# Cross-attention and mixture of experts on one core: two of four batches go sorted through DRAM and meet only their chosen experts, and all expert work moves to 128-token tiles with the weights as the moving operand

## The reference, cut to what matters

```python
# attention, per batch
q = ctx @ Wq.T + bq;  k = ctx @ Wk.T + bk            # 256x128 each
att = softmax(q @ k.T, axis=-1)                       # 256x256
x = x + layernorm(x) @ att.T
# experts, per token of all 4 batches
hs = layernorm(x)
probs = softmax(hs @ router_gate.T)                   # 8 experts
score, idx = top_k(probs, 2);  score /= sum(score)
inter = hs @ expert_gate_up[e]                        # 256 -> 256: gate and up interleaved
h = inter[1::2] * silu(inter[0::2])                   # 128
x = x + sum over the two chosen e: score_e * (h @ expert_down[e])
```

## Time and profile before

| | us |
|---|---|
| three runs | 113.2, 113.69, 115.03 |
| profiled execution | 112.85 |
| its span | 111.0 |
| PE busy | 99.6 (90% of the span) |
| DVE busy | 75.5 |
| ACT busy | 42.8 |
| POOL busy | 43.4 |
| DMA moved | 10.23 MB |

### The profile page before, as it was taken

How to read it: one execution, slowest core, us unless ns; L and a number is a source line. 1 busy time by engine, 2 the same in 40 slices (tenths; PEclk the granted TensorE clock), 3 DMA queues, 4 the chain that set the end, 5 groups by cost and what they waited for, 6 DMA issues and landing times.

```text
span 111.0 us, 1638 instructions
## 1 busy us (share of the span) xinstructions
PE 99.6 (90%) x544; PEld 82.2 (74%) x544; DVE 75.5 (68%) x196; ACT 42.8 (39%) x89; POOL 43.4 (39%) x46
## 2 busy tenths in 40 slices
PE   6997899559998839999999999999999999999960
PEld 6884585346876637988988787898998998988950
DVE  1169969879965299989999599728963563553750
ACT  3355986745346244642090603234033033034200
POOL 3005045527000419999279360740440440440400
PEclk9999999999999995899999999999999999999998
DMA  2999993000003980000000000397050000000005
GB/s 67 264 265 336 361 348 113 0 0 0 6 0 111 320 334 0 6 0 0 0 0 0 0 0 4 127 360 279 0 189 0 6 0 0 0 0 0 0 5 184
DMA packets 8167, 10.23 MB, mean 92 GB/s; under 512 B 712, under 2 KB 7120, under 8 KB 8160
## 3 DMA queue, kind: packets, MB, share of 16 engines
q1 hardware_dynamic: 7744, 9.81, 26.9%
q10 hardware_dynamic: 416, 0.33, 0.9%
HBM read 9.05 MB, written 1.08 MB: 91 GB/s over the span
## 4 chain that ended last, share of the span: by engine, by line
PE 77%; DVE 9%; DMA 5%; ACT 4%; issue 1%; POOL 1%; DVEq 0%; ACTq 0%
PE ps_g L462 21%; PE ps_u L462 20%; PE ps_out L487 20%; DMA score_bc<-score_rows 4%; PE ps_out L440 3%; ACT probs L540 2%; PE ps_out L402 2%; PE ps_a L381 2%; DVE hs L643 2%; DMA score_rows<-scoresT 1%; DVE stats L628 1%; DVE x_sb L798 1%; DVE x_sb L683 1%; PE ps_u L373 1%; PE ps_u L421 1%
## 5 line engine op out<-in xcount | busy, mean ns | idle before, releaser
L341 POOL TENSOR_TENSOR h_lo<-h,h_hi 128x512 fp32r<-128x512 f32 x15 | 20.2, 1348 | 33.9 <-ACT h_hi L584 33.9
L808 DVE SCALAR_TENSOR_TENSOR scaled<-tanh_g,score_bc 128x512 f32<-128x512 f32 (+1 forms) x17 | 13.0, 770 | 15.5 <-ACT tanh_g L592 10.2
L592 ACT ACTIVATE tanh_g<-ps_g 128x512 f32<-128x512 f32 (+1 forms) x17 | 9.6, 571 | 28.4 <-PE ps_g L462 28.3
L487 PE MATMUL ps_out<-down_hi,h_lo 128*128 128x256 f32 x64 | 18.2, 285 | 0.0
L487 PE MATMUL ps_out<-down_lo,h_hi 128*128 128x256 f32 x64 | 18.0, 281 | 0.0
L487 PE MATMUL ps_out<-down_hi,h_hi 128*128 128x256 f32 x64 | 17.8, 279 | 0.0
L311 POOL TENSOR_TENSOR gu_lo<-gu_raw,gu_hi 128x512 fp32r<-128x512 f32 x8 | 10.5, 1310 | 11.3 <-ACT gu_hi L516 11.3
L584 ACT CAST h_hi<-h 128x512 fp32r<-128x512 f32 (+1 forms) x17 | 10.0, 591 | 10.9 <-DVE h L821 9.2
L821 DVE TENSOR_TENSOR h<-ps_u,gated 128x512 f32<-128x512 f32 (+1 forms) x17 | 11.1, 660 | 2.3 <-DVE gated L814 0.5
L487 PEld LDWEIGHTS ps_out<-down_hi,h_lo 128*128 128x128 f32 x64 | 12.2, 190 | 0.7
L487 PEld LDWEIGHTS ps_out<-down_lo,h_hi 128*128 128x128 f32 x64 | 12.2, 190 | 0.6
(11 more groups left out here) (147 smaller groups left out, 159.4 us busy)
## 6 DMA issues: line engine op xcount, KB each, us to landing
score_bc<-score_rows SPq DMA_DIRECT2D x8, 512.0 KB, 5.5
gu_raw<-_ffn_expert_gate_up_dram SPq DMA_DIRECT2D x4, 512.0 KB, 8.3
down_raw<-n_L_ffn_expert_down_dram SPq DMA_DIRECT2D x2, 512.0 KB, 8.6
out_dram<-x_sb SPq DMA_DIRECT2D x4, 256.0 KB, 2.2
ctx_sb<-in_ctx_dram SPq DMA_DIRECT2D x2, 256.0 KB, 3.5
x_sb<-in_x_dram SPq DMA_DIRECT2D x1, 512.0 KB, 6.7
x_sb<-in_x_dram ACTq DMA_DIRECT2D x1, 256.0 KB, 3.9
x_sb<-in_x_dram SPq DMA_DIRECT2D x1, 256.0 KB, 3.6
```

Source lines behind the costliest of these rows:

```text
L341: nc.gpsimd.tensor_tensor(h_lo[:, U % 2], h[:, U % 2], h_hi[:, U % 2].bitcast(f32), ALU.subtract).then_inc(h_lo_ready, 1)
L487: last = nc.tensor.matmul(dst, a[:, U % 2, cols], w[:, e], start=(e == 0 and i == 0 and j % 2 == 0), stop=(e == E - 1 and i == 2), skip_gr ...
L592: nc.scalar.activation(tanh_g[:, U % 2, part], ps_g[U % 2][:, part], ACT.Tanh, scale=0.5).then_inc(tanh_ready, 1)
L808: nc.vector.scalar_tensor_tensor(out=scaled[:, part], in0=tanh_g[:, U % 2, part], scalar=1.0, in1=score_bc[:, U // E, U % E, part], op0=AL ...
```

## The change

Batches 2 and 3 stay dense. Batches 0 and 1 (512 tokens, 4 tiles of 128) are sorted. After routing, TensorE counts for each token how many earlier tokens chose the same expert ("R": a strictly triangular and an all-ones matrix times the choices), DVE makes a row number for each token and choice, and 8 indirect DMAs of POOL scatter the rows of hs to `xs_rows` in DRAM. Every expert's rows begin at a tile of 128, so 15 tiles hold all 1,024 rows whatever the routing. SP loads the tiles, PE transposes them, and each tile meets the weights of the one expert that its number gives: PE reads 15 expert numbers into registers and addresses `W` by them. Results go to `ys_rows` in DRAM, 8 indirect DMAs of POOL gather them for each token, and DVE adds the two weighted rows (`combine`).

All expert work is now in groups of two 128-token tiles. The tokens are the stationary operand, and 256 columns of weights (gate beside up) move. The result has tokens on the partitions, so a dense score is a scalar per partition and the broadcast through DRAM is gone; but h has to be transposed before down (`transpose_h`). There are 24 groups: experts 0 to 3 of batches 2 and 3, then 8 groups of sorted tiles (the last has one tile), then experts 4 to 7 of both batches. Down of group k runs behind gate and up of group k+2, and the transposes of h(k+1) behind that.

The attention of all four batches now runs batch by batch ahead of the first expert group, except for H and the logits of batch 3. The logits come with tokens on the partitions from eight matmuls of 16 columns per batch. The remainders of down move from DVE and POOL to POOL alone.

```diff
+        FILLS = ["wq", "wk", "C0", "Q0", "K0", "C1", "E0", "Q1", "K1", "C2", "E1", "X0", "Q2", "K2", "C3", "A0", "E2",
+                 "gate", "M0", "X1", "A1", "Q3", "K3", "M1", "E3", "X2", "A2", "H0", "M2", "L0", "H1", "X3", "A3", "L1",
+                 "M3", "H2", "R", "L2", "H3", "L3"]
...
+        GROUPS = ([("dense", e, 2) for e in range(4)] + [("dense", e, 3) for e in range(4)]
+                  + [("sorted", s, None) for s in range(SG)]
+                  + [("dense", e, 2) for e in range(4, E)] + [("dense", e, 3) for e in range(4, E)])
...
+            def down_split(e):
...
+                nc.gpsimd.tensor_copy(W[:, e, 4], down_raw[:, e]).then_inc(down_hi_ready, 1)
+                pool.wait_ge(down_hi_ready, e + 1)
+                nc.gpsimd.tensor_tensor(W[:, e, 5], down_raw[:, e], W[:, e, 4].bitcast(f32),
+                                        ALU.subtract).then_inc(down_lo_ready, 1)
...
+            for j in range(ST):
+                for r in range(2):
+                    nc.gpsimd.indirect_dma_start(
+                        out=xs_rows, out_offset=bass.IndirectOffsetOnAxis(ap=slot[:, r, j:j + 1], axis=0),
+                        in_=hs[:, j], in_offset=None).then_inc(rows_scattered, 16)
+            for e in range(4, E):
+                gu_lo_part(e)
+                down_split(e)
+            for i in range(2):
+                pool.wait_ge(ys_stored[i], 16 * len(range(i, SG, 2)))
...
+            def load_experts():
+                pe.wait_ge(tile_expert_ready, 1)
+                for i in range(SLOT_TILES):
+                    experts.append(pe.value_load(tile_expert[0:1, i:i + 1], min_val=0, max_val=E - 1))
...
+                for t in range(group_tiles(k)):
+                    e = expert(k, t)
+                    terms = [(lo, half, c) for lo, half in ((0, 1), (0, 0), (1, 0)) for c in range(NT)]
+                    for i, (lo, half, c) in enumerate(terms):
+                        if kind == "dense":
+                            a = (hsT_hi, hsT_lo)[lo][:, b, c, t * P:(t + 1) * P]
+                        else:
+                            a = (xsT_hi, xsT_lo)[lo][:, n % 2, c, t]
+                        last = nc.tensor.matmul(dst[:, t * N:(t + 1) * N], a, W[:, e, 2 * half + c],
+                                                start=(i == 0), stop=(i == len(terms) - 1))
...
+            for k in range(NG + 2):
+                if k < NG:
+                    s = k + 1 - FIRST_SORTED
+                    if 0 <= s < SG:
+                        transpose_rows(s)
+                    gate_up_group(k)
+                if k == 0:
+                    att("H3")
+                if k == 1:
+                    att("L3")
+                if k >= 2:
+                    down_group(k - 2)
+                if 1 <= k <= NG:
+                    transpose_h(k - 1)
...
+            def combine(j):
+                dve.wait_ge(yg_in[j], 32)
+                nc.vector.scalar_tensor_tensor(out=part[:, j], in0=yg[:, 0, j], scalar=w_top[:, j, 0:1], in1=x1_sb[:, j],
+                                               op0=ALU.mult, op1=ALU.add).then_inc(part_ready, 1)
...
+            att("M0")
+            normalise_probs(2)
+            neg_mean_rstd(3)
+            att("K3")
+            normalise_x1(0)
+            att("M1")
+            att("E3")
+            att("H0")
+            normalise_x1(1)
+            normalise_probs(3)
+            att("M2")
+            att("L0")
+            att("H1")
+            normalise_x1(2)
+            att("L1")
+            route_sorted()
+            att("M3")
+            att("H2")
+            normalise_x1(3)
+            place_rows()
+            att("L2")
+            route_dense(1, 2)
```

More of the change, by code:

```diff
@@ new lines, in cross_attention_moe_kernel @@
+        w_is_top = sb("w_is_top", [P, 2, T - ST, E])
+        scores = sb("scores", [P, T - ST, E])
+        chosen = sb("chosen", [P, ST + 1, E])
+        over = sb("over", [P, E, E, ST])
+        first_tile = sb("first_tile", [P, E])
+        place = sb("place", [P, ST, E])
+        own_place = sb("own_place", [P, 2, ST, E])
+        slot_f = sb("slot_f", [P, 2, ST])
+        tile_expert_f = sb("tile_expert_f", [1, SLOT_TILES])
+        slot = sb("slot", [P, 2, ST], u32)
+        began = sb("began", [1, SLOT_TILES, E - 1])
@@ L613, in _ @@
-            split_h(UNITS - 1)
+            gap_exp(0, slice(0, ST))
+            split_gu(3)
+            hs_hi(2)
+            gap_exp(1, tiles(2))
+            for e in range(4, E):
+                split_gu(e)
+            for k in range(NG + 2):
+                s = k + 1 - FIRST_SORTED
+                if 0 <= s < SG:
+                    xt_hi(s)
+                if k == 1:
+                    hs_hi(3)
+                if k < NG:
+                    tanh(k)
+                if k == 2:
+                    gap_exp(2, tiles(3))
+                s = k - 2 - FIRST_SORTED
+                if 0 <= s < SG:
+                    evict_ys(s)
+                if 1 <= k <= NG:
+                    ht_hi(k - 1)
@@ new lines, in route_dense @@
+            def route_dense(i, b):
+                ts, ds = tiles(b), slice((b - SB) * LT, (b - SB + 1) * LT)
+                choose(ts, LT)
+                weights(i, ts, 0.5)
+                for r in range(2):
+                    step_on(nc.vector.tensor_tensor(w_is_top[:, r, ds], is_top[:, r, ts],
+                                                    w_top[:, ts, r:r + 1].broadcast_to([P, LT, E]), ALU.mult))
+                joined()
+                nc.vector.tensor_tensor(scores[:, ds], w_is_top[:, 0, ds], w_is_top[:, 1, ds], ALU.add).then_inc(scores_ready, 1)
@@ new lines, in _ @@
+            step_on(nc.vector.tensor_copy(tile_id[:], tile_no[:]))
+            step(nc.vector.tensor_copy(thr[:], thr_no[:]))
+            for e in range(E):
+                last = nc.vector.memset(thr[:, e, e:E], 1.0e6)
+                step_on(last)
+            joined()
+            att("gate")
+            att("M0")
[4 more added lines that the diff above has]
+            att("M1")
+            att("E3")
+            att("H0")
```

1202 lines of the change are left out of this document (611 added, 591 removed), and 4 rows, old and new, of the table FILLS.

## The result

The changed kernel takes **148.65 us** (median of 4 runs, 146.8 to 149.22) against 113.91 (113.2 to 115.03) for the kernel before in the same session: ratio 1.310, 95% interval 1.302 to 1.318. The direction was forecast, the size was not: 148.65 lies above the range of 121 to 143. The profiled execution took 149.22 us with a span of 147.4.

The account below looks back on a forecast made before the run. TensorE, busy 99.6 of 111.0 us, was taken as the bound. First group at 48.5 + PE's work 62.4 + 4.85 + 1.6 + 6.1 + 1.0 + 1.7 + 4.4 = 130.6, plus 1.85: 132.4 us; range 121 to 143.

Parts of the forecast that it names:

- the first group: Start of expert work on PE, after four batches' attention: 48.5 us, between 35.3 and 52.
- PE's work: PE's matmuls and transposes from the first group on: 62.4 us, with 4 row transposes per sorted tile.
- The register loads: 15 loads of expert numbers on PE's queue: 0.3 us each, 4.5 us, 6.1 with the clock's fall.
- The first rival: Register loads are dear, 0.85 us each, 12.8 us in all: 140.7 us; chance 0.2.
- The hole at the second group: PE idle ahead of the second group's down while DVE routes batch 3: 2.0 us.
- the upper bound of the front: Latest start of the first expert group, with DVE slowed beside POOL: 52 us.
- The hole ahead of the logits of batch 3: PE idle while DVE routes batch 2 and finishes H3's remainder: 2.85 us.
- The clock: PE's slower clock after idle: 1.6 us after the first two holes, 1.6 more at the register loads.
- third rival: Waits ahead of the experts are absent, first group at 35.3: 119.2 us; chance 0.08.
- register instructions between matmuls: 90 register instructions in PE's sorted tiles: 1 us taken, from 0 to 5.4.
- after PE: From PE's end to the span's end, a combination in place of an add: 4.4 us.
- The second rival: Indirect DMAs are dear, 1.77 us each, delaying the final gathers by 3.3 us: 135.7 us; chance 0.08.

Follow-up runs that it names:

- The static version: Changed kernel with the 15 expert numbers written into the program, so no register loads: 135.37 us.
- experiment 3: Changed kernel with POOL's weight splits for experts 4 to 7 held until batch 3 is routed: 141.33 us.
- both with busy matmuls in the sorted form: Unread matmuls added in three places of the changed kernel, 155.64 us; in one hole of the version with POOL's last splits held, 152.31 us.
- five loads in the hole: Changed kernel with five register loads ahead of the second group's second matmuls, then one in each of ten groups: 144.77 us.
- POOL's and ACT's order: Changed kernel with POOL's 1/sqrt ahead of the weight splits and ACT's X2, A2 and H0 ahead of batch 3's exponentials: 144.54 us.
- both combinations: Changed kernel with POOL's 1/sqrt first, its last splits held and register loads taken apart: 137.02 us; with ACT's reordering too: 130.53 us.
- the spread one: Changed kernel with register loads issued two at a time behind each sorted group's row transposes: 140.95 us.
- the two edits of POOL alone: Changed kernel with POOL's 1/sqrt ahead of the weight splits, 143.85 us; separately, with POOL's last splits held, 141.33 us.

## Why the prediction was wrong, point by point

**Direction and the first group.** Right in kind: the waits, their order and their names were as forecast, and the largest term after PE's work was the start of the experts. It came 5.9 us late. 2.1 of it is the half clock at 6.29, 1.1 is `is_top` of the sorted half (1.39 us at 47.45, POOL's split at 47.51, in place of the 0.29 of the kernel before), 0.8 the logits of batch 2 at half clock, and 1.9 is the rest, which was not taken apart.

**The register loads: the step that failed first.** The forecast took 0.3 us for each, 0.2 for the word and two instructions at 0.05. Both parts were too small: the load took 0.30 and what goes with it 0.38, 0.68 in all. The hole was 9.06 against 4.5, and the clock behind it cost 2.7 against 1.6. The first rival had this mechanism at 0.85 us each and 140.7. The static version, 13.3 us shorter, 1.8 of which lie in its earlier start, shows that this one place cost some 11.5 us, where the forecast had 6.1.

**The hole at the second group: the step that failed second.** Forecast 2.0, measured 4.13, because DVE's routing of batch 3 was priced at undisturbed durations and POOL's splits ran beside it. The forecast had seen the row of 1.71 against 0.73 and put contention only into the upper bound of the front. Holding POOL back made it 1.17. The hole ahead of the logits of batch 3 was overestimated by 1.0.

**The clock: the step that was mis-sized most.** The forecast had 3.2 us, taken from one hole. It was 10.7: 8.0 up to 84.3 and 2.7 behind the loads. The first group itself started at half clock (PE had been busy 4.9 of the 10.0 us before it), and each of the next two holes was followed by half clock again, up to 68.7 and 78.9. The 10.7 is an estimate from the windows; the experiments show 2.7 of it behind the loads and 2.1 behind the second hole. The other 5.9 are not confirmed by an edit: the attempt to buy back such a part by filling a hole gave nothing.

**PE's work: a wrong count, in the other direction.** "4 transposes of its rows" per sorted tile are two: the tile has two blocks of 128 columns. The trace after has 30 records where the forecast counted 60:

```profile
L468 PE MATMUL bank<-ident,xin x30: 272/273/472, 93.4 to 115.5; 128*128 128x128 f32 x30
```

At 0.109 each that is 3.3 us too many in the sum. Without this error the forecast would have been 129.1, further off, so the error brought it nearer by luck. One slip changes no result: for late gathers the forecast points to its third rival, and they stand in its second.

**Accounting.** Front +5.9, PE's work -3.3, first hole -1.0, second hole +2.1, loads +4.6, clock +7.5, register instructions between matmuls -1.0 (they are hidden), holes in the last groups +0.9, after PE -0.3, and +1.4 as the rest, groups a little over their sum: +16.8 of span, 130.6 to 147.4.

**What was right.** Dense groups of 2.3 us. The scatters and gathers, forecast at 1.2 us, are issued every 1.27, and neither the zeroing nor the gathers delay the end. The end after PE is 4.1 us against 4.4. The second rival's effect did not come.

**Rivals.** The first was the nearest (140.7), 8 us below what was measured. None had three causes at once, and the forecast treated the loads, the contention and the clock as independent small terms, while a hole also bears on the clock of what follows it: those of 1.86, 4.13 and 9.06 us were each followed by half clock, and the 1.17 of experiment 3 was not.

## What to carry to other kernels

When work is pulled ahead of the busy stage, price PE's later work at the clock that its earlier idleness leaves. That is most of the 7.5 us missed here. A value that PE needs in a register costs 0.68 us of its queue, so one at a time between groups of 2.3 to 2.7 us is free here and 15 in a block are not. Steps of DVE on a critical hand-over should not run beside POOL's long two-operand instructions; holding POOL back cost one line and gave 5 to 6 us.

## What the hardware did that was not expected

- DVE's pair of operations on 128x16 waited a whole POOL instruction: 0.26 became 1.56 beside one of 1.30, and was 0.26 again with POOL idle.
- ACT stood still 1.2 to 6.2 us at a time, during scatters, gathers or both, in the profiled executions of six kernels: both with busy matmuls in the sorted form, five loads in the hole, POOL's and ACT's order, and both combinations. It did not in the changed kernel, the static one, the spread one and the two edits of POOL alone, which have the same DMAs, nor in the kernels that have none. Leaving the indirect DMAs out ended it and gave 9.8 us. Why they stop ACT in one program and not in another is open. In the five that were hit during the scatters PE's granted clock stood at full when ACT stopped; in the others it was at full for only some 3 us of the scatters (in the changed kernel from 58.4 to 61.8). That alone is not the reason, since during the gathers the clock was at full in the kernels that were not hit too.
